# Projections in another order on every engine, inputs in long rows, and loads of difference blocks ahead of later writes in a fused attention and expert kernel

## The reference

```python
x = x + tanh(g_xattn) * xattn(layernorm(x), ctx, ctx, frac)   # 16 heads of 16
x = x + tanh(g_ffn) * ffn(layernorm(x))                       # 8 experts, top 2, and a shared one
# inside xattn, per sequence and head:
D = clip(frac[None, :] - frac[:, None], -0.2, 0.2)
attn = gamma * (Q @ K.T) / 4 + delta * (alpha_pos * max(D, 0) + alpha_neg * min(D, 0))
out = softmax(attn) @ V
```

## Time and profile before

| | |
|---|---|
| median of 3 runs | 525.38 us (525.08 to 526.19) |
| the profiled execution | 526.24 us, its span 524.4 us |
| busy share of the span | PE 90%, DVE 71%, ACT 62%, POOL 47% |
| mean granted TensorE clock | 0.963 of full |

### The profile page before, as it was taken

One profiled execution on the slowest core, in us unless ns is written; L12 is line 12 of the kernel. 1 busy time (PEld: TensorE's weight loads), 2 busy tenths in 40 slices (PEclk: granted clock), 3 DMA queues, 4 the chain that ended last, 5 costly groups with the idle time before them and its releaser, 6 DMA issues.

```text
span 524.4 us, 17381 instructions
## 1 busy us (share of the span) xinstructions
PE 474.4 (90%) x6343; PEld 401.0 (76%) x6359; DVE 370.6 (71%) x897; ACT 322.6 (62%) x890; POOL 245.0 (47%) x277
## 2 busy tenths in 40 slices
PE   3799678898989998999999989999999999999990
PEld 1566457787878885666667979999999999999980
DVE  5876475988888897589896767666666666666650
ACT  2885576998989998766776554544534445445330
POOL 4467476787885566368781022322322223223231
PEclk9799697999999999999999989999999999999995
DMA  7702127367565438413247642232232222322211
GB/s 263 267 2 71 36 64 212 92 153 209 141 190 161 128 117 322 201 61 122 86 130 165 233 113 47 40 60 40 44 58 40 54 46 40 60 40 45 36 23 20
DMA packets 48551, 55.49 MB, mean 106 GB/s; under 512 B 17138, under 2 KB 39666, under 8 KB 48372
## 3 DMA queue, kind: packets, MB, share of 16 engines
q1 hardware_dynamic: 41348, 45.44, 28.8%
q0 software_dynamic: 7152, 9.34, 9.8%
HBM read 35.95 MB, written 18.82 MB: 104 GB/s over the span
## 4 chain that ended last, share of the span: by engine, by line
PE 66%; ACT 9%; POOL 8%; DMA 6%; DVE 4%; issue 3%; SPq 1%; DVEq 0%; POOLq 0%; ACTq 0%
PE bank L1292 61%; ACT W L738 4%; DMA W<-d_dram 3%; PE bank L1387 3%; PE bank L1556 2%; POOL W L609 2%; ACT W L744 1%; DMA xres<-xs_dram 1%; DMA W<-ctxT 1%; POOL W L589 1%; POOL W L601 1%; DVE st L917 1%; ACT W L760 1%; POOL rstd L552 1%; DVE xres L945 1%
## 5 line engine op out<-in xcount | busy, mean ns | idle before, releaser
L884 ACT ACTIVATE hbuf<-bank,b1t 128x128 f32<-128x128 f32 x312 | 88.8, 368 | 111.9 <-PE bank L1292 107.1
L674 POOL DMA_INDIRECT out<-xres,idu x39 | 61.0, 1564 | 177.8 <-DVE xres L1264 175.0
L1292 PE MATMUL bank<-W,xT 128*128 (+1 forms) x1704 | 138.7, 252 | 0.0
L1292 PEld LDWEIGHTS bank<-W,xT 128*128 128x128 bf16 (+1 forms) x1704 | 115.4, 98 | 12.7
L1292 PE MATMUL bank<-xres,W 128*128 128x128 bf16 (+1 forms) x1916 | 122.8, 223 | 0.7 <-issue 0.5
L1292 PEld LDWEIGHTS bank<-xres,W 128*128 (+1 forms) x1920 | 112.2, 98 | 7.6 <-issue 2.2
L738 ACT ACTIVATE W<-bank,mx 128x128 f32<-128x128 f32 x256 | 69.4, 394 | 3.9 <-DVE mx L963 3.9
L1292 PE MATMUL bank<-W 128*128 128x17 bf16 (+2 forms) x1376 | 59.7, 189 | 12.4 <-DMA W<-d_dram 5.5
L1292 PEld LDWEIGHTS bank<-W 128*128 128x128 bf16 x1376 | 51.1, 98 | 20.6 <-DMA W<-d_dram 7.4
L1245 DVE TENSOR_TENSOR xT<-hbuf,xT 128x512 bf16<-128x512 f32 x78 | 54.0, 693 | 2.7
L1292 PE MATMUL bank<-W,hsplit 128*128 128x256 bf16 x432 | 54.7, 277 | 0.0
(11 more groups left out here) (151 smaller groups left out, 599.4 us busy)
## 6 DMA issues: line engine op xcount, KB each, us to landing
stage<-wts SPq DMA_DIRECT2D x26, 512.0 KB, 4.1
W<-wts SPq DMA_DIRECT2D x10, 512.0 KB, 7.7
xres<-xs_dram SPq DMA_DIRECT2D x39, 128.0 KB, 2.1
xs_dram<-hbuf SPq DMA_DIRECT2D x6, 774.0 KB, 6.5
W<-d_dram SPq DMA_DIRECT2D x32, 128.0 KB, 3.7
W<-ctxT SPq DMA_DIRECT2D x4, 512.0 KB, 6.3
xres<-x SPq DMA_DIRECT2D x4, 512.0 KB, 7.5
d_dram<-W SPq DMA_DIRECT2D x16, 128.0 KB, 3.2
```

The costliest lines, as they stand in the source:

```text
L674: nc.gpsimd.indirect_dma_start(out, bass.IndirectOffsetOnAxis(idu[:, par, t:t + 1], axis=0), ysb[par][t], None, compute_op=ALU.add).then_i ...
L884: ins = nc.scalar.activation(hbuf[:, q, c * TR:(c + 1) * TR], bank[UPS * par + q][:, c * TR:(c + 1) * TR], ACT.Gelu, bias=b1t[:, par, UC * ...
L1292: return nc.tensor.matmul(o, a, b, start=start, stop=stop, **kw)
```

## The change

Five edits. The host lays `x`, the context and the projection weights out so that each partition reads one run of DRAM (4 KB, 4 KB and 2 KB where it was pieces of 1 KB, 2 KB and 1 KB); bytes and order of these issues stay. On PE the first group's value projection comes before its transposes, with the biases after it. On POOL `slopes` move from behind `deviation4(3)` to ahead of `context_low(2)`, `deviation4(2)` goes behind `clip(0)` and `clip(1)`, and `clip(2)` ahead of `deviation4(3)`. On ACT the differences go ahead of `queries_high` in groups 1 and 2, and in group 0 `weight_high(0)` ahead of `inputs_high`; on DVE `weight_low(0)` goes ahead of `inputs_low`. On SyncE `load_difference(b)` comes first in the loop.

```diff
-                sp.dma_start(ctf[g % 2].rearrange("p (c t) -> p c t", c=DC),
-                             ctxT[:, :, g * T4:(g + 1) * T4].rearrange("c p t -> p c t")).then_inc(ld_ct[g % 2], 16)
+                sp.dma_start(ctf[g % 2], ctxT[g]).then_inc(ld_ct[g % 2], 16)
...
             for b in range(2, B):
+                load_difference(b)
                 if b + 2 < B:
                     write_difference(b + 2)
                 if b + 7 < B:
                     load_frac(b + 7)
                 load_piece(b // 2, b % 2)
-                load_difference(b)
...
             context_low(1)
+            slopes()
             context_low(2)
-            deviation4(2)
             pool.wait_ge(ld_col, 16)
             clip(0)
             clip(1)
+            deviation4(2)
             context_low(3)
             split_difference(0)
             split_difference(1)
+            clip(2)
             deviation4(3)
-            slopes()
-            clip(2)
             clip(3)
...
+                if 1 <= g < Q4 - 1:
+                    difference_high(2 * g - 2)
+                    difference_high(2 * g - 1)
                 if g == Q4 - 1:
                     exponent(0)
                     exponent(1)
                 for o in range(DC):
                     queries_high(g, o)
-                if g >= 1:
+                if g == Q4 - 1:
                     difference_high(2 * g - 2)
-                if 1 <= g < Q4 - 1:
-                    difference_high(2 * g - 1)
...
             for g in range(Q4):
+                if g == 0:
+                    weight_low(0, 2)
                 for c in range(DC):
                     inputs_low(g, c)
-                if g == 0:
-                    weight_low(0, 2)
...
             project_keys(0)
-            turn_inputs(0)
+            project_values(0)
             pe.wait_ge(rows_ready, 1)
             for o in range(DC):
                 bias_keys(o)
-            project_values(0)
+            for s in range(4):
+                bias_values(s)
+            turn_inputs(0)
             project_queries(0)
```

More of the change, by code:

```diff
@@ L363, in load_x @@
             def load_x(k):
-                sp.dma_start(xres[:, k * 4 * D:(k + 1) * 4 * D].rearrange("p (b d) -> p b d", d=D),
-                             x[4 * k:4 * k + 4].rearrange("b p d -> p b d")).then_inc(ld_x[k], 16)
+                sp.dma_start(xres[:, k * 4 * D:(k + 1) * 4 * D], x[k]).then_inc(ld_x[k], 16)
             def load_proj(k):
-                sp.dma_start(wst_at(k).rearrange("p (c d) -> p c d", d=D),
-                             wproj[k].rearrange("(c p) d -> p c d", p=P)).then_inc(ld_wp[k], 16)
+                sp.dma_start(wst_at(k), wproj[k]).then_inc(ld_wp[k], 16)
             def load_ctx(g):
@@ L788, in _ @@
             for g in range(Q4):
-                for c in range(DC):
-                    inputs_high(g, c)
                 if g == 0:
@@ L793, in _ @@
                     act.wait_ge(ld_cst, 16)
+                for c in range(DC):
+                    inputs_high(g, c)
                 for o in range(DC):
@@ L1328, in value_bank, with bias_values @@
                 return bank[6 + s // 2][:, (s % 2) * D:(s % 2 + 1) * D]
+            def bias_values(s):
+                ins = mm(value_bank(s), oneb[:], brows[:, 2 * D:3 * D], False, True, skip_group_check=True)
+                if s % 2:
+                    ins.then_inc(v_ps, 1)
             def project_values(g):
@@ L1339, in project_values @@
                                skip_group_check=True)
-                    ins = mm(value_bank(s), oneb[:], brows[:, 2 * D:3 * D], False, True, skip_group_check=True)
-                    if s % 2:
-                        ins.then_inc(v_ps, 1)
+                    if g:
+                        bias_values(s)
             def project_queries(g):
@@ L1660 @@
     f = np.float32
-    x = a("x")
-    ctxT = np.ascontiguousarray(a("ctx_1024").reshape(N, D).T.reshape(DC, P, N))
+    x = a("x").reshape(Q4, 4, P, D).transpose(0, 2, 1, 3).reshape(Q4, P, 4 * D)
+    ctxT = a("ctx_1024").reshape(Q4, T4, DC, P).transpose(0, 3, 2, 1).reshape(Q4, P, DC * T4)
     frac = np.ascontiguousarray(a("fside_BxS2_0").reshape(1, N))
-    wproj = np.stack([a(f"L0_xattn_W{k}").T for k in "qkvo"])
+    wproj = np.stack([a(f"L0_xattn_W{k}").T.reshape(DC, P, D).transpose(1, 0, 2).reshape(P, DC * D) for k in "qkvo"])
     brow = np.concatenate([a(f"L0_xattn_b{k}") for k in "qkvo"]).reshape(1, 4 * D)
```

## The result

The changed kernel takes **510.5 us** as a median (509.2 to 511.6, four runs); the kernel before, beside it, took 525.2 us (524.6 to 526.2, four runs). The ratio is **0.9717** (95% interval 0.9687 to 0.9747). The forecast was 510.0 us, range 507 to 518. Some executions of every kernel here, changed or not, take over 1.5% longer than its fastest; the times and ratios of the experiments leave them out.

A forecast was written before the change was run, and what follows sets the result against it. The prediction took a queue of matmuls on TensorE (66% of the chain) as the bound, with PE's stops and their clock as what could change. Terms summed to 15.5 us, from 525.4 to 509.9, predicted as 510.0 us; range 507 to 518.

The forecast's parts named there:

- First stop: PE's idle before the first scores: moving slopes behind it ends ACT's waits for POOL's clips, saving 4.3 us.
- Its clock: After the first scores, PE no longer runs at the lower clock from 58.5 to 67.5 us, saving 3.7 us.
- Second stop and its clock: At sequence 2, PE's wait for difference loads goes, 3.5 us; the low clock and lag behind it, 1.7 us.
- Later sequences: Eight sequences from 97.29 us take 65.3 instead of 67.14 us once the load queue is cured: 1.9 us.
- Long rows: The first context load lands sooner with longer DRAM rows, and the engines behind it start earlier: 0.4 us.
- PE's start: Value products fill PE's first idle, up to 3 us lead, but it ends at deviation4(2): 0 us.
- Behind the attention: What follows the attention loop is released by its end and shifts as a whole, with no gain of its own.
- (a): Rival: the first stop stays because ACT meets another wait between 40 and 50 us; 518.0 us, chance 0.12.
- (b): Rival: difference loads of even sequences queue behind padding and a piece, so later sequences wait; 517 us, chance 0.10.
- (c): Rival: slopes slowed by overlap with DVE's work at the start delay deviation4(2); 512 to 514 us, chance 0.08.
- (d): Rival: PE's lead at the start survives, ACT not being gated by deviation4(2); 507 us, chance 0.05.
- (e): Rival: slower than before, SyncE's new wait at load_difference delaying writes and ACT each round; 531.9 us, chance 0.03.

The follow-up runs named there:

- e1: Kernel before with only SyncE's edit, load_difference(b) first in the loop: 521.4 us, ratio 0.9897.
- e10: The same kernel as e1 (kernel before with only the loads moved), profiled once more: 518.4 us, a single execution.
- e3: Kernel before with only the long rows for x, the context and the projection weights: 525.0 us, ratio 0.9955.
- e4: Kernel before with only the first group's edits on PE, ACT and DVE (values ahead of transposes, weight_high(0) and weight_low(0) first): 526.6 us, ratio 1.0005.
- e2: Kernel before with only POOL's new order (clips, deviation4, slopes) and ACT's new places for difference_high: 519.4 us, ratio 0.9860.
- e5: The changed kernel again, unaltered, to stand beside its variants: 511.5 us, ratio 0.9701 to the kernel before.
- e8: Changed kernel with load_difference(b) behind the write and the frac load but still ahead of load_piece: 512.0 us, ratio 0.9743.
- e9: Changed kernel with the first group's old order on PE, ACT and DVE: 511.5 us, ratio 0.9702.
- e12: The changed kernel once more, unaltered, as neighbour of other runs: 511.9 us, ratio 0.9746 to the kernel before.
- e7: Changed kernel with deviation4(2) between clip(0) and clip(1): 508.6 us, ratio 0.9671.
- e11: Changed kernel with deviation4(2) between clip(0) and clip(1), run once more: 510.2 us, ratio 0.9693.
- e6: Changed kernel with the slopes put back between deviation4(3) and clip(3): 516.8 us, ratio 0.9823.

## Why the prediction was right

Opening times on PE, both profiled executions; the last column is the lead of the changed kernel.

| | before | after | lead |
|---|---|---|---|
| first scores | 58.49 | 54.08 | 4.41 |
| end of the query projections | 67.73 | 59.96 | 7.77 |
| sequence 2 | 80.49 | 69.05 | 11.44 |
| sequence 4 | 97.29 | 84.62 | 12.67 |
| sequence 12 | 164.43 | 150.36 | 14.07 |
| end of the span | 524.4 | 509.8 | 14.6 |

**First stop, 4.3 us forecast.** The chain was right at each step: no wait in `difference_high`, `inputs_high(3)` at 48.60 (forecast 49.1), first scores at 54.08 (54.2). The lead of 4.41 us compares two executions whose `norm4(2)` didn't start together. Counted from that start, all profiled executions agree (us; the last column is from `norm4(2)` to the end of the query projections):

| | `norm4(2)` | to the first scores | to the end of the queries |
|---|---|---|---|
| old order on POOL and ACT: before, e1, e10, e3, e4 | 30.77 to 32.64 | 25.85 to 25.87 | 35.1 to 36.3 |
| new order: after, e2, e5, e8, e9, e12 | 32.02 to 32.94 | 21.70 to 21.72 | 27.6 |
| `deviation4(2)` between the clips: e7, e11 | 31.86, 30.98 | 21.72 | 27.6 |
| slopes back: e6 | 31.26 | 24.97 | 35.4 |

So the cure itself is worth 4.1 us, of which the slopes are 3.25. But the same edits hold `deviation4(2)` behind two clips: `norm4(2)` starts 1.4 us after the end of the statistics in the old order and 2.2 to 3.5 us after it in the new one. Against e3, which has the old order and the long rows as well, the first scores of the changed kernel come only 2.3 to 2.9 us sooner.

**Its clock, 3.7.** From the first scores to the end of the queries it is 9.24 to 10.40 us with the stop and 5.88 without: 3.4 to 4.5. The stop and its clock together are 7.5 to 8.7, where 8.0 was forecast.

**Second stop and its clock, 3.5 and 1.7.** The lead grows by 3.67 us to sequence 2 and by 1.23 to sequence 4. The second was a little high: the difference conversions on ACT pace this sequence too. e8 shows which part of SyncE's queue it was.

**Later sequences, 1.9.** Eight took 65.74 us where 67.14 stood, 1.4 less; forecast 65.3. The loads alone did not give even that (68.8 and 67.6 in e1 and e10), since the stop of 1.5 to 1.8 us in the loop and the clock behind it ate it. That stop has 0.51 us in the profiled execution of the changed kernel. It isn't cured: in e9 it has 1.63 us and the eight sequences take 68.0.

**Long rows, 0.4.** The size is not settled, and I had set it too low. The first matmul came 1.09 us earlier (7.26 and 8.35), and alone the edit gave 1.4 us by the medians and 2.4 (0.8 to 3.9) by the ratio. I had only two transfers with other neighbours, and took their difference. Where the gain sits stays open: in e3 `norm4(2)` starts 0.7 to 1.9 us earlier than in the kernels with the old order and the old rows, and by sequence 12 nothing of it is left. In the changed kernel the clips ahead of `deviation4(2)` hold it up. The Trainium skill, page "DMA: Bandwidth & Descriptors", section "Specifications", puts the least size for the full rate at 512 B; here rows above that bound still gained a third in rate when they became 2 and 4 KB long, so the measurement decides against it.

**PE's start, 0.** Right in its sum: `deviation4(2)` came at 31.01 where I had 31.3, and e4 and e9 give 1.0005 and no difference. The lead that I expected hardly existed. In e9, with the old start, PE turns group 1 at 21.62, in the three executions of the changed kernel at 20.77 to 21.57; What the value products win, PE loses again in the first group: it idles 1.81 us at 17.52 for `inputs_low(0)` of DVE (1.94 in e4). So most of PE's lead ends there and not at `deviation4(2)`. The slopes ran from 20.52 to 25.05, and `context_low(2)` starts at 25.05, as forecast.

**Behind the attention, nothing.** From sequence 12 to the end 359.97 us stood and 359.4 stand. That they are so near is luck. The lead sinks to 10.7 us at 283.49: a group of six 128x512 matmuls near 188 us took 2.62 us at the lower clock (1.46 elsewhere), and PE waits 1.07 us at 283.49. It comes back near 305 us of the kernel before, where PE waited 2.23 us for a routed tile and the matmuls behind it took 4.33 us instead of 2.78. That wait is 1.40 us in e5 and 0.56 in e12. From sequence 12 to the end the profiled executions take 357.5 to 360.8 us (e7's apart, at 365.4), whatever the edit, so no term under 3 us can be read from there.

The terms measured: 4.41 + 3.36 + 3.67 + 1.23 + 1.40 + 0.5 = 14.6 us against 15.5. The parts alone add up to the whole: 1.03% (e1) + 1.40% (e2) + 0.45% (e3) - 0.05% (e4) = 2.83%, and the change gives 2.83%. So close an agreement is luck too: each interval is 0.3 to 0.6% to either side.

**The rivals.** (a) did not come; e6 shows what it would have cost: a ratio of 0.982, where the 518.0 that I gave it is 0.986. (b) did not: no wait of PE for the differences is left. (c) did not as written: the slopes took 4.5 us in their new place. But POOL's new order does hold `deviation4(2)` up, by 0.8 to 2.1 us against the old one, through the clips. (d) did not: PE came 1.6 us sooner past the wait, but ACT is gated by `deviation4(2)`, and the first scores follow ACT. (e): the wait is there, 24.9 us of it, and harmless, since no one needs SyncE meanwhile.

**Signs that I had wrong.** I wanted a clock above 0.95 in every ten microseconds from 20 us on, and no stop over 2 us between 34 and 60. PE stopped 3.53 us ahead of 34.49, and the window from 30 to 40 has 0.83:

```profile
30.00:40.00 10.00, 6.47 (x29) 3.65 (x28) 5.80 (x10) 7.63 (x16) 5.83 (x8) 0.83 0.00 1
```

I had reasoned that the lead is lost at `deviation4(2)`, and not gone on: a lead that is lost is a stop of PE, and a stop can have a clock. Here that costs 0.9 us in the turn (1.97 against 1.04) and 0.5 in the first group behind it (1.99 against 1.46), but only on PE. The first scores don't feel it. Rows of ACT and PE in e9, where PE stopped 2.97 us at the same place and kept its clock:

```profile
32.59 2.07 ACT L757 ACTIVATE W<-xres,nmr,rstd 128x256 f32<-128x256 f32 x4 [3.90 <-POOL nmr L550]
...
34.72 1.09 PE L1304 MATMUL bank<-cst,W 128*128 128x128 f32 x8 [2.97 <-ACT W L757]
...
54.29 0.63 PE L1290 MATMUL bank<-W 128*128 128x64 bf16 x16 [0.68 <-issue]
```

From `norm4(2)` to the scores it is 21.70 us here and 21.71 in the changed kernel, whose turn ran at the lower clock. The term of 0 held because the chain runs through POOL, ACT and DVE and not through PE. In e11 the scores come 1.16 us before e12's because `norm4(2)` does (30.98 and 32.14), and not because the clock stays up.

## What to carry to other kernels

Price a stop of TensorE with what follows it: here a first stop of 4.1 us cost 7.5 to 8.7, and both stops were put there by something small that stood ahead of something urgent in an in-order program (slopes needed 10 us later; a wait for a piece ahead of a load). Before counting a lead of one engine, find which engine the next milestone follows: PE's start bought nothing, since the first scores follow `norm4(2)` on ACT, and POOL's clips ahead of `deviation4(2)` were the next thing to move. Measure from a shared milestone and not from the start: two executions of one kernel (e1 and e10) start `norm4(2)` 0.7 us apart, and from there to the first scores they differ by 0.02. First loads gain from long rows; what they are worth in the end was not settled here.

## What the hardware showed that I had not expected

**A stop without a releaser.** In the slot ahead of sequence 4 PE halts once in the middle of a group: 0.58 us before, 0.51 after, 1.76 in e1, 1.48 in e10, 1.63 in e9. The timelines of before and after:

```profile
93.73 0.55 PE L1292 MATMUL bank<-W 128*128 128x64 bf16 x13 [0.58 <-issue]
```

```profile
86.88 0.51 PE L1290 MATMUL bank<-W 128*128 128x17 bf16 x14 [0.51 <-issue]
```

One of the 35 packets of the queue "instruction" (q8) starts 0.8 to 2.3 us ahead of each of these stops (in e1 between 93.5 and 94.0, and the stop begins at 94.4). The end of the stop follows the packet more closely than its beginning: in the twelve profiled executions with a stop in this slot, 0.19 to 1.76 us long, it ends 2.4 to 2.9 us after the start of the packet. That PE waits there for its next instructions would fit. This is argued; no run tested it, and why the place goes with the order of the loads stays open.

**How short a stop can cost the clock, and how long a stop need not.** In e1 the stop of 1.76 us was followed by 6 us at half clock, and so were 1.48 us (e10) and 1.63 us (e9) by 3 us of it each, while 0.51 to 1.24 us at the same matmul in seven other executions were followed by none. Ahead of the turn of group 2 the clock fell behind 2.38 us (e5) and 3.53 us (after), and not behind 2.97 us (e9) and 3.00 us (e2). So the length of the stop alone doesn't decide. The Trainium skill, page "TensorE: Matmul & The Clock Gate", section "HAM oscillation", warns of the price of idle time; the rows here agree for a stop this short in a loop where PE also has many small gaps.

**The granted clock of the start.** The record reads 1.00 from 7 to 11 us, but twelve 128x512 matmuls take 4.08 us there, 0.34 each, where six take 1.46 later, 0.24 each. The profile gives one of them 621 ns as a mean from 7.5 to 9.3 us, 456 from 9.3 to 11, and 379 from 42.8 on. At the start the matmuls themselves are the better witness.
